# One 128-column transpose for the combine weights of four token tiles, and their copy, store and spread laid out by tile and expert

## The reference

```python
def gate(x2d, gate_kernel, gate_bias):                       # routing
    scores = sigmoid(x2d @ gate_kernel) + gate_bias          # (n, 16)
    group_sum = sum(top2 of each group of 4)                 # (n, 4)
    masked = where(group is one of the best 2, scores, 0)
    w, idx = top_k(masked, 4)
    return idx, w / (sum(w) + 1e-20) * 2.5

x = x + attention(layernorm(x))                              # window of 64
xn = layernorm(x)
combine = einsum('nke,nk->ne', onehot(idx), w)               # (n, 16), 4 not zero
g, u = einsum('nh,ehm->enm', xn, w_gate), einsum('nh,ehm->enm', xn, w_up)
y_e = einsum('enm,emh->enh', silu(g) * u, w_down)
y = einsum('ne,enh->nh', combine, y_e)
out = x + y + shared_expert(xn)
```

## Time and profile before

| | |
|---|---|
| three runs, us | 690.54, 691.94, 690.07; median 690.54 |
| the profiled execution, us | 691.06, of which 689.3 is its span |
| busy share: PE, PE weight loads, DVE, ACT, POOL | 95%, 75%, 85%, 76%, 72% |
| granted TensorE clock, mean | 0.999 of full speed |
| hardware DMA queue | 50208 packets, 52.14 MB, 24.5% of 16 engines |

### The profile page before, as it was taken

The page is one execution under the profiler, slowest core; times in us unless marked ns, Lnnn a source line. Parts: engine busy times, 40 slices in busy tenths (PEclk is TensorE's granted clock), DMA queues, the critical chain, the costliest instruction groups (busy, mean ns, idle before and its releaser), DMA issues.

```text
span 689.3 us, 19513 instructions
## 1 busy us (share of the span) xinstructions
PE 655.5 (95%) x6232; PEld 518.2 (75%) x6232; DVE 585.1 (85%) x1710; ACT 521.0 (76%) x1603; POOL 496.0 (72%) x635
## 2 busy tenths in 40 slices
PE   3999889999999999999999999999999999989996
PEld 2877767777777787777777787777787777767775
DVE  3598898989989898989989898989989898888664
ACT  2786788787878878788887979787887879763432
POOL 3504267788888787878888787878888787776533
PEclk9999999999999999999999999999999999999999
DMA  5010032140414132140413123040313213041321
GB/s 180 1 33 31 2 96 78 40 148 5 143 41 124 61 100 85 35 127 24 136 46 124 61 78 106 23 131 30 127 57 115 69 63 108 13 134 33 117 80 47
DMA packets 50245, 52.60 MB, mean 76 GB/s; under 512 B 5664, under 2 KB 31904, under 8 KB 50080
## 3 DMA queue, kind: packets, MB, share of 16 engines
q1 hardware_dynamic: 50208, 52.14, 24.5%
HBM read 43.20 MB, written 4.72 MB: 70 GB/s over the span
## 4 chain that ended last, share of the span: by engine, by line
PE 61%; DVE 14%; ACT 12%; issue 6%; POOL 4%; DMA 1%; DVEq 0%; POOLq 0%; ACTq 0%; SPq 0%
PE PS L1091 11%; PE PS L947 8%; PE PS L909 8%; PE PS L911 7%; PE PS L910 7%; ACT probs L635 6%; PE PS L1038 4%; ACT q_by_head L590 4%; DVE neg_max L818 3%; PE PS L935 3%; PE PS L1061 3%; PE PS L1051 2%; PE PS L977 2%; DVE sums L784 2%; DVE probsT L774 2%
## 5 line engine op out<-in xcount | busy, mean ns | idle before, releaser
L635 ACT ACTIVATE probs<-PS,neg_max 128x96 f32<-128x96 f32 (+1 forms) x1024 | 248.0, 361 | 83.1 <-DVE neg_max L818 82.9
L513 POOL TENSOR_TENSOR gate<-gate,spread 128x512 f32<-128x512 f32 x124 | 158.4, 1277 | 85.0 <-ACT gate L590 39.1
L518 POOL TENSOR_TENSOR hh<-gate,tu 128x512 f32<-128x512 f32 x108 | 139.3, 1289 | 15.7 <-DVE tu L807 8.6
L1091 PE MATMUL PS<-wd,hh 128*128 128x128 f32 x1024 | 138.1, 278 | 4.2 <-POOL hh L518 2.1
L1091 PEld LDWEIGHTS PS<-wd,hh 128*128 128x128 f32 x1024 | 126.4, 191 | 13.3 <-issue 5.8
L818 DVE TENSOR_REDUCE neg_max<-PS 128x4 f32<-128x384 f32 (+1 forms) x256 | 121.7, 514 | 15.5 <-PE PS L947 15.0
L807 DVE SCALAR_TENSOR_TENSOR tu<-th,PS 128x512 f32<-128x512 f32 x128 | 87.1, 681 | 47.5 <-ACT th L606 40.9
L909 PE MATMUL PS<-x_hi,w_hi 128*128 128x512 f32 x288 | 125.0, 434 | 0.3 <-DVE tu L807 0.3
L774 DVE STREAM_TRANSPOSE probsT<-probs 128x768 f32<-128x768 f32 (+1 forms) x128 | 114.5, 894 | 0.0
L606 ACT ACTIVATE th<-PS 128x512 f32<-128x512 f32 x128 | 81.9, 640 | 43.0 <-PE PS L911 41.4
L911 PE MATMUL PS<-x_lo,w_hi 128*128 128x512 f32 x288 | 114.2, 396 | 0.0
(11 more groups left out here) (107 smaller groups left out, 990.0 us busy)
## 6 DMA issues: line engine op xcount, KB each, us to landing
spread<-weights_by_expert SPq DMA_DIRECT2D x248, 128.0 KB, 2.9
X<-x SPq DMA_DIRECT2D x32, 256.0 KB, 3.5
OUT<-H SPq DMA_DIRECT2D x16, 256.0 KB, 3.1
out<-OUT SPq DMA_DIRECT2D x16, 256.0 KB, 3.7
ffn_stage<-w_gu SPq DMA_DIRECT2D x1, 1152.0 KB, 6.5
wd<-w_down SPq DMA_DIRECT2D x1, 512.0 KB, 6.6
weights_by_expert<-cT SPq DMA_DIRECT2D x16, 32.0 KB, 1.6
probsT<-w_att SPq DMA_DIRECT2D x1, 192.0 KB, 3.0
```

The lines of the kernel that those rows point to most:

```text
L513: tt(gate2[:, :], gate[:, k % 2, :], spread[:, k % SP_BUFS, :], ALU.mult).then_inc(s_g2, 1)
L518: tt(hh[:, k % 2, :], gate2[:, :], tu[:, k % 2, :], ALU.mult).then_inc(s_h, 1)
L635: ins = nc.scalar.activation(probs[:, u % PROB_BUFS, tt, 2 * rows + e, j0:KW], PS[:, rows, n * KW + j0:n * KW + KW], ACT.Exp, bias=neg_max ...
L1091: ins = mm(PS[:, 7, r], hh[:, k % 2, r], wd[:, k, :], start=(k == 0 and n == 0), stop=(k == NP - 1), skip_group_check=True)
```

## The change

`comb` gets 8 blocks of 16 columns instead of 4, of which the last 4 are set to zero once; so it is 128 columns wide, and one full 128x128 transpose takes the place of four. Row 16n + e of its result is expert e of tile n. The copy `cT` has 64 partitions (tile, expert) x 128 tokens instead of 16 x 512, the store writes 64 rows of 512 bytes, and a spread DMA reads for each of its 64 partitions four pieces of 512 bytes, one per tile, 8 KB apart, instead of one of 2 KB. `pick` becomes 64 x (4 x 4 x 64), and where TensorE repeats the rows it does four products of 128 columns instead of one of 512. Three waits on GpSimd's counter of the start go up by one for the new memset.

```diff
@@ tiles @@
-        comb = sb("comb", [P, NT, E])
-        cT = sb("cT", [E, TOK])
-        pick = sb("pick", [E, 4, M])
+        comb = sb("comb", [P, 2 * NT, E])
+        cT = sb("cT", [NT * E, P])
+        pick = sb("pick", [NT * E, NT, 4, M])
-        weights_t = nc.dram_tensor("weights_by_expert", (2, E, TOK), F32, kind="Internal").ap()
+        weights_t = nc.dram_tensor("weights_by_expert", (2, NT * E, P), F32, kind="Internal").ap()
@@ SyncE, spread_out @@
                 for e in range(2):
-                    sp.dma_start(spread[M * e:M * e + M, k % SP_BUFS, :],
-                                 weights_t[g.par, 2 * k + e].partition_broadcast(M)
+                    row = weights_t[g.par].rearrange("(n e) t -> e n t", n=NT)[2 * k + e]
+                    sp.dma_start(spread[M * e:M * e + M, k % SP_BUFS, :].rearrange("p (n t) -> p n t", n=NT),
+                                 row.partition_broadcast(M)
                                  ).then_inc(s_spread[k % SP_BUFS], 16)
@@ GpSimd @@
+            nc.gpsimd.memset(comb[:, NT:2 * NT, :], 0.0).then_inc(s_pool, 1)
-            pool.wait_ge(s_pool, 5)
+            pool.wait_ge(s_pool, 6)
-                        which = ident[0:E, 0:4].unsqueeze(2).broadcast_to([E, 4, M])
-                        tt(pick[:, :, :], which, which, ALU.mult).then_inc(s_pick, 1)
+                        which = ident[0:NT * E, 0:NT * E].rearrange("p (n e) -> p n e", n=NT)[:, :, 0:4]
+                        which = which.unsqueeze(3).broadcast_to([NT * E, NT, 4, M])
+                        tt(pick[:, :, :, :], which, which, ALU.mult).then_inc(s_pick, 1)
-                        tt(comb[:, :, :], kept[:, :, :], w_sum[:, :].unsqueeze(2).broadcast_to([P, NT, E]),
+                        tt(comb[:, 0:NT, :], kept[:, :, :], w_sum[:, :].unsqueeze(2).broadcast_to([P, NT, E]),
                            ALU.mult).then_inc(s_cb, 1)
@@ ScalarE @@
-                            copy(cT[:, :], bank[0:E, :], scale=0.5 * ROUTE_SCALE).then_inc(s_taken[side], 1)
+                            copy(cT[:, :], bank[0:NT * E, 0:P], scale=0.5 * ROUTE_SCALE).then_inc(s_taken[side], 1)
@@ TensorE @@
-                            mm(PS[:, k, :], pick[:, 2 * k:2 * k + 2, :].rearrange("p e m -> p (e m)"),
-                               cT[:, :], start=True, stop=True).then_inc(s_wp, 1)
+                            for n in range(NT):
+                                ins = mm(PS[:, k, P * n:P * n + P],
+                                         pick[:, n, 2 * k:2 * k + 2, :].rearrange("p e m -> p (e m)"),
+                                         cT[:, :], start=True, stop=True)
+                            ins.then_inc(s_wp, 1)
-                        for n in range(NT):
-                            ins = nc.tensor.transpose(bank[0:E, P * n:P * n + P], comb[:, n, :], ident)
-                        ins.then_inc(s_filled[side], 1)
+                        nc.tensor.transpose(bank[:, 0:P], comb[:, :, :].rearrange("p n e -> p (n e)"), ident
+                                            ).then_inc(s_filled[side], 1)
```

More of the change, by code:

```diff
@@ L479, in slot @@
                                                 ALU.add).then_inc(s_cst, 1)
-                        pool.wait_ge(s_pool, 8)
+                        pool.wait_ge(s_pool, 9)
                         pool.wait_ge(s_cst, 3)
@@ L651, in slot @@
                         if g.fixed and g.n == 0:
-                            act.wait_ge(s_pool, 7)
+                            act.wait_ge(s_pool, 8)
                         side, bank = filled(act, sl, s, LATE)
```

## The result

The changed kernel takes 714.8 us (median of 715.01, 709.15, 714.59 and 717.12), the kernel before 690.3 on the same chip: ratio 1.033 (1.031 to 1.036). Forecast was 689.6 us with a range of 687.1 to 691.9. The profiled execution took 715.01 us with a span of 713.2 and a mean granted clock of 0.986 (before 0.999).

The account below looks back on a forecast made before the run. The prediction took DVE's `tu`, which holds TensorE's gate product, to bound the loop. Terms of -0.3, -0.15, -0.65 and +0.15 summed to -0.95 us, taking 690.54 to 689.6 us, range 687.1 to 691.9.

Parts of the forecast that it names:

- the term of the spread: Spread DMAs with 256 pieces for 64: a pair lands 0.1 us later, covered in the loop, worth 0.0.
- The floor of the Trainium skill: About 10.5 ns per packet, 2.7 us per spread DMA, 43 us per group; set aside, given 0.01 of the 0.05.
- Rival B: Spread: a piece of 512 bytes costs the 97 ns of a 2 KB one; about 700 us, chance 0.05.
- the cover: Loop slack for a later spread: 0.23 us from the copy, 0.40 before the down product, 1.03 before DVE's maxima; 1.66 in all.
- the transposes: Loop groups 1 to 12: one transpose ends about 0.33 us earlier, but TensorE then waits for `tu`; worth 0.0.
- rival A: Each transpose counts in the loop and drain: -5.3 us, 685.2; smaller form 687.1; chance 0.12 for both.
- this term: ScalarE's copy `cT` in the loop: 0.23 us shorter, 0.02 passed on per group, times 12: -0.3 us.
- the split product: Rows repeated by TensorE, 4 places: 8 records of 128 columns for two of 512, 0.04 us more each; +0.15 us.
- rival C: Weight loads of 64 rows don't hide behind TensorE's products of 128 columns; 692.4 us, chance 0.06.
- The single transpose: Drain, groups 14 and 15: one transpose takes 0.11 us where four take 0.44; -0.65 us for both groups.
- the other terms: All but the spread in the loop: copy -0.3, group 13 -0.15, drain -0.65, repeated rows +0.15; sum -0.95 us.
- rival D: Nothing passes on at all, the drain's 0.33 us being lost in another wait there; 690.5 us, chance 0.07.

Follow-up runs that it names:

- e4: Changed kernel, each spread DMA reading 64 different rows of x in four pieces of 512 bytes instead of one row of weights for all partitions; 690.95 us.
- e5: Changed kernel with the four tiles' rows of one expert 8.5 KB apart in DRAM instead of 8 KB; 692.6 us.
- e8: Kernel before, a row's four pieces of 512 bytes laid 4 KB apart and the rows of two experts 16.5 KB apart; 693.6 us.
- e16: Changed kernel, each spread DMA reading 64 different rows of x in steps of 8 KB, one per partition, each four times; 710.4 us.
- e1b: Repeat: changed kernel with rows ordered by expert and tile, so the spread reads whole 2 KB rows; 691.0 us against 691.6, ratio 0.9984.
- e9b: Changed kernel with the tiles' rows of one expert 9 KB apart instead of 8 KB, run with an interval; 690.8 us against 691.6, ratio 0.9989.
- e1: Changed kernel with rows ordered by expert and tile, so the spread reads whole 2 KB rows; 691.3 us against 691.5, ratio 0.9990.
- e2: Kernel before, with each row of weights laid in DRAM as four pieces of 512 bytes, 1 KB apart; 695.1 us, ratio 1.005.
- e7: Kernel before, with weights laid out in DRAM as the changed kernel has them, pieces of 512 bytes 8 KB apart; 711.3 us, ratio 1.029.
- e15: Changed kernel, each spread DMA reading four rows of x 8 KB apart, each for all 64 partitions, instead of the weights; 716.4 us.

## Why the prediction was wrong

**The step that failed** is the term of the spread: "I take +0.1 us for a pair's landing, between -0.3 (the shorter pieces pipeline better) and +0.6", and from it "covered ... Worth 0.0". Measured: +2.1 us, by 256 reads of one place at 11.1 ns for 64, and 1.0 us per slot of it was not covered. I had priced a piece by the loads of x as the nearest row of the same size. Size was the wrong likeness: a load of x reads 256 KB side by side, so its pieces don't fall on one place, and e4 shows that a spread that reads like this is as cheap (2.9 us). The row that was near in kind was the spread itself, whose single DMA ran at one piece each 11.1 ns; read in slices of 0.1 us it would have said that four times the pieces may take four times as long.

**The floor of the Trainium skill that I set aside.** In the stretches above a lone spread passed a piece each 11.1 ns in both kernels. The Trainium skill, "DMA: Bandwidth & Descriptors", section Bandwidth, gives about 10.5 ns per packet; by that rule a DMA of 256 packets takes 2.7 us, an estimate from the skill's page, and the trace of the changed kernel, with 2.84, agrees. But 9 KB apart the same 256 pieces land in 3.1 us, 0.2 us above the 64 of before, so here it is no floor of a packet. Nor do the DMAs of a group add up to the 43 us that I worked out from the skill's page: a slot of the changed kernel takes 40.06 us, and behind the first DMAs of a group the rate rises to 108 GB/s and more.

**Rival B** had the sign, the place (GpSimd's wait for the first pair, TensorE waiting for `hh`) and by luck the size of the delay (2.3 us for the 2.1 of the landing); I gave it 0.05. Its reason, 97 ns of engine time per piece, was wrong: the share of the DMA engines rose from 24.5% to 29.1% only. Its 700 us were too low for two reasons. Its cover was 1.66 us, so 0.66 per slot; a steady slot lost 1.03. The first two terms of the cover, 0.23 and 0.40, fit: 2.1 less 0.63 is 1.5, and TensorE waited 1.4 to 1.5 us for `hh` in these slots. It was the third, 1.03 us ahead of DVE's maxima, of which only some 0.4 was there. The runs between agree with a cover of about 1.0 in all: slots of e5 and e8 with landings of 3.4 and 3.5 us are unchanged, those of e16 with 4.7 us lose 0.9 (39.94 on the mean for 39.03). And it had no term for the clock, 7 to 9 us.

**What held.** The load of L912 waits for `tu` 0.57 us in the slots of the loop, 0.6 forecast for 0.30:

```profile
418.05 0.19 PEld L912 LDWEIGHTS PS<-x_hi,w_hi 128*128 128x128 f32 x1 [0.57 <-DVE tu L810]
418.19 0.28 ACT L593 ACTIVATE cT<-PS 64x128 f32<-64x128 f32 x1
```

So the transposes are worth nothing in the loop, and rival A has fallen: where nothing else changed (e1b, e9b) the slots of the loop are 0.05 to 0.07 us shorter on the mean, not 0.33. `cT` takes 0.28 us for 0.34 forecast; the -0.05 to -0.07 us per slot stand for the -0.02 of this term, though no run has the copy alone. In the drain of e9b the split product has

```profile
633.15 1.08 PE PS L998 x8
```

1.08 us per place for 1.05, +0.04 forecast; so rival C has fallen. The single transpose takes a place of 0.11 us in that drain, as forecast. `pick` took 1.9 us for 2.4 and nobody waited. Where the spread is about as cheap as before, the whole of the other terms, forecast as ratio 0.9986, measured 0.9990 (e1, 0.9976 to 1.0003), 0.9984 (e1b, 0.9972 to 0.9996) and 0.9989 (e9b, 0.9974 to 1.0003). Only e1b's interval leaves out 1, and by little, so rival D (0 us) is hardly told from the forecast by these.

## What to carry to other kernels

A DMA that cuts rows into pieces is priced by where its pieces lie: when many partitions read the same few rows, count the reads per address modulo 8 KB (as these runs show it for rows within some 500 KB), and keep rows that are read together off that distance; 1 KB of padding, or another order of the rows, won 22 to 25 us here. Price a changed DMA by the row of the same DMA, seen alone in flight in fine slices, and not by another of the same piece size. And where a wait ahead of TensorE grows by 1 us or more, look whether what stands behind it runs at half the clock: in e2 1.45 us of delay cost 3.3. Such a fall isn't certain, and the same kernel has it in one execution and not in another.

## What the runs showed that I had not expected

- One place in DRAM served one read each 11.1 ns: 46 GB/s in pieces of 512 bytes, 184 GB/s in pieces of 2 KB. Places repeat each 8 KB (8 and 16 KB apart: landings of 4.9 to 5.8 us; 4 KB: 3.5), but four rows 512 KB apart are four places (3.1 us).
- A lone DMA of the kernel before passes its pieces at the same 11.1 ns, which pieces of 2 KB hide.
- Waits of TensorE for `hh` of 2.5 to 3.0 us were followed in e2 and, three times out of four, in the changed kernel by 3 to 7 us at half of the clock. In e7 waits of 2.52 and 3.01 us were not: the eight products behind them took 1.13 us. And one of 1.71 us in e15 was (2.03 us for the eight). So the length of the wait alone doesn't decide it here. The rows are of the changed kernel and of e7, both in the slot of group 13:

```profile
629.30 2.05 PE L1097 MATMUL PS<-wd,hh 128*128 128x128 f32 x8 [2.99 <-POOL hh L521]
```

```profile
625.32 1.13 PE L1092 MATMUL PS<-wd,hh 128*128 128x128 f32 x8 [3.01 <-POOL hh L519]
```
